# A joint activation-table set, doubled slot buffers, and half of one shared group moved behind the first experts

## The reference, cut to what matters

```python
x = x + tanh(g_xattn[0]) * attention(_layernorm(x), ctx)      # 16 heads, quantised, all 2048 tokens
x = x + tanh(g_ffn[0])   * moe0(_layernorm(x))                # 32 experts, 4 per token, shared part of width 704
x = x + tanh(g_xattn[1]) * wkv(time_decay, time_first, _layernorm(x), ctx)
x = x + tanh(g_ffn[1])   * moe1(_layernorm(x))                # 8 experts, 2 per token, shared part of width 352
```

## Time and profile before

| | us |
|---|---|
| median of 3 runs | 1297.46 (1297.25 to 1297.59) |
| the profiled execution | 1299.77 |
| its span, first to last instruction | 1298.0 |
| TensorE busy | 1081.6 (83% of the span) |
| VectorE busy | 969.6 (75%) |
| ScalarE busy | 899.4 (69%) |
| GpSimd busy | 696.8 (54%) |

### The profile page before, as it was taken

How to read it: one execution, slowest core, us unless ns; L and a number is a source line. 1 busy time by engine, 2 the same in 40 slices (tenths; PEclk the granted TensorE clock), 3 DMA queues, 4 the chain that set the end, 5 groups by cost and what they waited for, 6 DMA issues and landing times.

```text
span 1298.0 us, 24037 instructions
## 1 busy us (share of the span) xinstructions
PE 1081.6 (83%) x8245; PEld 631.3 (49%) x8360; DVE 969.6 (75%) x1781; ACT 899.4 (69%) x1537; POOL 696.8 (54%) x610
## 2 busy tenths in 40 slices
PE   6958888888888888888888875998998697798992
PEld 4623444444444444444444653565544254456771
DVE  6999899999999999999999567233235687643334
ACT  4649899999999999999999653144406465533441
POOL 3016988887887888788787615276301000462331
PEclk9969999999999999999999977999999898699996
DMA  5686787888897888886676454199431021123335
GB/s 173 125 143 127 155 179 161 158 176 169 165 173 164 171 165 181 167 170 124 114 115 108 73 167 135 31 278 265 159 121 65 0 79 55 41 85 98 97 97 205
DMA packets 388191, 176.36 MB, mean 136 GB/s; under 512 B 329805, under 2 KB 373042, under 8 KB 388072
## 3 DMA queue, kind: packets, MB, share of 16 engines
q1 hardware_dynamic: 381368, 157.84, 55.7%
q0 software_dynamic: 6480, 16.77, 3.9%
q10 hardware_dynamic: 224, 0.20, 0.0%
HBM read 52.70 MB, written 43.59 MB: 74 GB/s over the span
## 4 chain that ended last, share of the span: by engine, by line
PE 42%; DVE 31%; ACT 10%; issue 7%; DMA 5%; POOL 4%; SPq 1%; POOLq 0%; DVEq 0%; ACTq 0%
DVE top L368 20%; PE bank L217 7%; PE bank L231 7%; ACT weight L411 6%; PE bank L2340 4%; PE bank L1081 3%; DMA answered_rows<-yrow,target 3%; PE bank L249 3%; PE bank L1064 3%; PE bank L2356 2%; PE bank L1068 2%; PE bank L1721 1%; PE bank L267 1%; DVE x_sb L2028 1%; POOL weight L463 1%
## 5 line engine op out<-in xcount | busy, mean ns | idle before, releaser
L411 ACT ACTIVATE weight<-bank,bias,sq_all 128x1024 uint8<-128x1024 f32 x512 | 610.0, 1200 | 32.4 <-PE bank L231 27.2
L368 DVE TENSOR_REDUCE top<-bank 128x1 f32<-128x512 f32 (+1 forms) x683 | 610.8, 951 | 16.1 <-PE bank L217 5.0
L463 POOL CAST weight<-turned 128x2048 bf16<-128x2048 uint8 x256 | 478.9, 1892 | 45.2 <-PE bank L249 24.7
L231 PE MATMUL bank<-kT,query 128*128 128x512 bf16 x915 | 285.7, 384 | 26.2 <-ACT weight L411 12.2
L249 PEld LDWEIGHTS bank<-v_sb,weight 128*128 128x128 bf16 x4096 | 172.1, 97 | 109.7 <-POOL weight L463 7.4
L217 PE MATMUL bank<-kT,qspace 64*128 64x512 bf16 x687 | 138.1, 395 | 63.2 <-DVE top L368 63.2
L249 PE MATMUL bank<-v_sb,weight 128*128 128x16 bf16 x4096 | 172.6, 170 | 6.3 <-POOL weight L463 5.9
L217 PE MATMUL bank<-kT,query 128*128 128x512 bf16 x331 | 127.0, 384 | 2.1 <-DVE top L368 1.4
L1697 POOL DMA_INDIRECT dispatched_rows<-qspace,put x32 | 33.9, 1060 | 152.6 <-DVE qspace L2130 144.0
L231 PEld LDWEIGHTS bank<-kT,query 128*128 128x128 bf16 x1024 | 60.1, 97 | 104.2 <-ACT weight L411 60.6
L411 ACT ACTIVATION_READ_ACCUMULATOR weight<-bank,bias,sq_all 128x1 f32 x512 | 101.5, 198 | 0.0
(11 more groups left out here) (303 smaller groups left out, 1530.3 us busy)
## 6 DMA issues: line engine op xcount, KB each, us to landing
dispatched_rows<-zeros SPq DMA_DIRECT2D x32, 524.0 KB, 3.2
answered_rows<-zeros SPq DMA_DIRECT2D x16, 512.0 KB, 3.1
late<-answered_rows SPq DMA_DIRECT2D x16, 512.0 KB, 5.7
wgu<-in_L_ffn_w_gate SPq DMA_DIRECT2D x32, 176.0 KB
wgu<-in_L_ffn_w_up SPq DMA_DIRECT2D x32, 176.0 KB
wdn<-in_L_ffn_w_down SPq DMA_DIRECT2D x32, 176.0 KB
erow<-dispatched_rows SPq DMA_DIRECT2D x39, 131.0 KB
query<-qspace SPq DMA_DIRECT2D x32, 128.0 KB, 3.1
```

Source lines behind the costliest of these rows:

```text
L231: mm = pe.matmul(unit[u % 2][:, v * 512:(v + 1) * 512], query2[:, t % 2, h, :], kT[:, h // 2, first + v * 512:first + (v + 1) * 512], star ...
L368: ve.tensor_reduce(top[:, first:first + count], bank[:, first % 3:first % 3 + count, :], AX.X, ALU.max).then_inc(s_max, 1)
L411: ac.activation(weight8[:, n % BYTES, u * 1024:(u + 1) * 1024], unit[u], ACT.Exp, bias=bias[:, n:n + 1], scale=sq_all[:, n:n + 1], accum_o ...
L463: po.tensor_copy(weight[:, n % 3, :, :, :].rearrange("p c q two -> p (c q two)"), turned8[:, n % 3, :, :].rearrange("p c q -> p (c q)").bi ...
```

## The change

It has three parts.

1. `ac.preload_act_table_set("natural_log_exp_and_others")` is written into ScalarE's list at 14 places: once in the preparation behind the Tanh, twice in the front (behind chunks 0 and 1 of the shared part), eleven times in mixing, each behind the last Silu of a run. This set holds Ln and Exp both.
2. `marked` and `numbered` get a second buffer each, used in turn. `mark_slots(g)` waits for `table_products` g-1 instead of g, and from group 2 on only. `front_pool` does the same, and starts a group at `choices_marked` (the end of `choose`) instead of `destinations_ready` (the end of `place`).
3. Chunks 3 to 5 and the four answers of shared group 0 leave the front. They stand at the head of mixing now, before those of group 1, on TensorE, ScalarE and VectorE. The experts' TensorE list waits for `hidden_ready` 3 in place of `shared_answers_added` 4.

```diff
+            LOGS = "natural_log_exp_and_others"
@@ preparation, ScalarE
                     ac.activation(tgates[:], gates[:], ACT.Tanh).then_inc(s_prep_scalar, 1)
+                    ac.preload_act_table_set(LOGS)
                     triple(2)
@@ buffers
-            marked = late[:, 6, :].bitcast(BF16).rearrange("p (n s) -> p n s", s=P)
+            marked = [late[:, k, :].bitcast(BF16).rearrange("p (n s) -> p n s", s=P) for k in (6, 4)]
...
@@ front_pool
-                    po.wait_ge(sm_["destinations_ready"], g + 1)
-                    if g > 0:
-                        po.wait_ge(sm_["table_products"], g)
+                    po.wait_ge(sm_["choices_marked"], g + 1)
+                    if g >= 2:
+                        po.wait_ge(sm_["table_products"], g - 1)
@@ front_tensor
                 fill_table(3)
-                hidden0(0, 3, 6)
-                pe.wait_ge(sm_["rows_chosen"], 1)
-                answers0(0)
@@ front_scalar
                 shared_scalar(ac, 0, 0, 1)
+                ac.preload_act_table_set(LOGS)
                 copy_logits(2)
...
                 shared_scalar(ac, 0, 1, 2)
+                ac.preload_act_table_set(LOGS)
                 copy_logits(3)
...
                 residuals(3)
-                shared_scalar(ac, 0, 3, 6)
@@ mark_slots
-                    else:
-                        ve.wait_ge(sm_["table_products"], g)
+                    if g >= 2:
+                        ve.wait_ge(sm_["table_products"], g - 1)
@@ front_vector
                 mark_slots(3)
-                hidden0(0, 2, 5)
+                hidden0(0, 2, 3)
                 take_table()
-                hidden0(0, 5, 6)
-                answers0(0)
@@ experts_tensor
-                    pe.wait_ge(sm_["shared_answers_added"], G)
+                    pe.wait_ge(sm_["hidden_ready"], 3)
@@ mixing_tensor
                         pe.wait_ge(sx_["answers_weighted"], E0)
+                        for c in range(3, NW0):
+                            hidden0(0, c)
+                        for k in range(G):
+                            answers0(0, k)
                         for c in range(NW0):
                             hidden0(1, c)
@@ mixing_scalar (the first and two of the other ten preloads)
+                        shared_scalar(ac, 0, 3, NW0)
                         shared_scalar(ac, 1, 0, NW0)
                         for c in range(4):
                             shared_scalar(ac, 2, c, c + 1)
+                        ac.preload_act_table_set(LOGS)
...
                         shared_scalar(ac, 3, 1, 3)
+                        ac.preload_act_table_set(LOGS)
                         inverse(1)
...
                         silu1(1, 2)
+                        ac.preload_act_table_set(LOGS)
                         copy_rows(2)
```

More of the change, by code:

```diff
@@ L1128, in program @@
             table = buffers(first_experts)
-            marked = late[:, 6, :].bitcast(BF16).rearrange("p (n s) -> p n s", s=P)
-            numbered = late[:, 7, 0:G * K0 * E0].bitcast(BF16).rearrange("p (n a e) -> p n a e", a=2, e=E0)
+            marked = [late[:, k, :].bitcast(BF16).rearrange("p (n s) -> p n s", s=P) for k in (6, 4)]
+            numbered = [late[:, 7, k * G * K0 * E0:(k + 1) * G * K0 * E0].bitcast(BF16).rearrange("p (n a e) -> p n a e", a=2, e=E0) for k in range(2)]
             slot_b, slot_n, lane, lane_n = table("slot_b", [P, P], BF16), table("slot_n", [P, P], U32), table("lane", [P, 1]), table("lane_n", [P, 1], U32)
@@ L1160, in front_pool @@
                 for g in range(NG):
-                    po.wait_ge(sm_["destinations_ready"], g + 1)
-                    if g > 0:
-                        po.wait_ge(sm_["table_products"], g)
+                    po.wait_ge(sm_["choices_marked"], g + 1)
+                    if g >= 2:
+                        po.wait_ge(sm_["table_products"], g - 1)
                     for k in range(G):
                         n = slice(k * K0, (k + 1) * K0)
-                        po.tensor_scalar(numbered[:, n, 0, :], hot[:, g % 2, n, :], float(g * G + k + 1), None, ALU.mult).then_inc(sm_["slots_numbered"], 1)
-                    po.tensor_scalar(numbered[:, :, 1, :], hot[:, g % 2, :, :], lane[:, 0:1], None, ALU.mult).then_inc(sm_["slots_numbered"], 1)
+                        po.tensor_scalar(numbered[g % 2][:, n, 0, :], hot[:, g % 2, n, :], float(g * G + k + 1), None, ALU.mult).then_inc(sm_["slots_numbered"], 1)
+                    po.tensor_scalar(numbered[g % 2][:, :, 1, :], hot[:, g % 2, :, :], lane[:, 0:1], None, ALU.mult).then_inc(sm_["slots_numbered"], 1)
             def front_tensor(pe):
@@ L1208, in fill_table @@
                     for n in range(G * K0):
-                        mm = pe.matmul(bank[:, 7, 0:2 * E0], marked[:, n, :], numbered[:, n, :, :].rearrange("p a e -> p (a e)"),
+                        mm = pe.matmul(bank[:, 7, 0:2 * E0], marked[g % 2][:, n, :], numbered[g % 2][:, n, :, :].rearrange("p a e -> p (a e)"),
                                        start=g == 0 and n == 0, stop=g == NG - 1 and n == G * K0 - 1)
```

2 lines of the change are left out of this document (1 added, 1 removed).

## The result

The changed kernel took **1285.42 us** (median of 4 runs, 1284.8 to 1285.71) against 1297.53 for the kernel before beside it: ratio **0.9902**, 95% interval 0.9885 to 0.9919. The forecast was 1285.8.

What follows compares the result with a forecast made beforehand. The prediction took a chain of waits to bound the kernel, through TensorE for 42% and VectorE for 31%. Front, experts and moved work -4.2 and mixing -7.5 sum to -11.7, off the median 1297.46: 1285.8 us, range 1280.5 to 1292.5.

Steps and rivals of the forecast that it cites:

- The front's first loads: End of attention to choose(1): two table loads (2.57 us) and one before group 3's Exp (1.28) leave the chain, -3.85 us.
- the prediction's estimate was 1273: Rival: each of nine loads on the chain also costs a drain of 1.4 us, about 1273 us; chance 0.01.
- The table: Front: with second buffers and the earlier loads the table is full at 801.2 against 810.06, -8.9 us (bounds -7 and -10.3).
- Table to experts: Full table to first expert: TensorE idles 4.5 us and 1.2 for two gathers, cold clock +1.3; experts start 27.5 us earlier.
- Behind the experts: Moved chunks (10.4 us) and answers (0.89 and 11.97) stand in full on TensorE's chain after the experts: +23.3 us.
- The front net: Front, experts and moved work together: -27.5 + 23.3 = -4.2 us.
- Mixing: Loads leave ScalarE's chain around inverse(1), inverse(2), inverse(3), other loads stood in waits: -7.5 us, bounds -3.5 and -11.
- the clock, which the forecast kept as a rival at -3: Rival: shorter TensorE gaps in mixing keep its clock up, 3 us more gained, 1282.8 us; chance 0.13.
- GpSimd does not pace the experts: Rival claimed the opposite: GpSimd's lost lead of six gathers (7.8 us) shows in full, 1293.6 us; chance 0.14.
- Mixing does not swallow the loads: Rival claimed the opposite: VectorE is next in line in mixing, -3.5 instead of -7.5, 1289.8 us; chance 0.18.
- The experts don't stay cold: Rival claimed the opposite: first experts stay at 1.2 GHz, up to 2.6 us each, kernel slower; chance 0.03.
- The set is kept: Rival claimed the opposite: Ln and Exp still get their own sets, 14 loads added, none saved, 1299.7 us; chance 0.03.

Runs made afterwards that it cites:

- Experiment 5, e6_scalar_numbers: Changed kernel with the wide product of group 3's numbers on ScalarE instead of GpSimd: 0.9908 of the kernel before.
- e8, experiment 7: Joint set and buffers without the move, chunk 3 done ahead of fill_table(3), VectorE's chunk 2 ahead of place(3): 0.9842 of the kernel before.
- e10: Joint set and buffers without the move, run beside the changed kernel in one session: 1304.36 us, 0.9880 of the kernel before.

## Why the prediction was right, by its own steps

The total held (1285.8 against 1285.42), and so did the split in its main lines; the term for mixing was too small, and a fall of the clock behind the experts hid most of that by chance.

- **The front's first loads**, -3.85: measured -4.0 at `choose(1)`. No drain of 1.4 us per switch shows: Ln at 741.49 comes with VectorE's statistics, and the start is 2.62 us earlier, 1.28 of its own, as one load of 1.283 says. By the Trainium skill (ScalarE: Activation LUTs, "What ACT_TABLE_LOAD costs"), which counts a drain with every switch, the prediction's estimate was 1273. The total of 1285.42 doesn't bear that out.
- **The table**, -8.9: measured -9.0, but the step inside was told the wrong way round. The forecast let VectorE's `mark_slots(3)` wait for GpSimd's wide product. In fact `mark_slots` ran undelayed (2.29) and GpSimd's product stretched from 1.56 to 3.69. As one full wait is one full wait, the table was full at the same time. Experiment 5 shows that it is this wait: without the product GpSimd no longer sets the end.
- **Table to experts**, 4.5 and 1.2 us exposed, clock +1.3: measured 4.61 and 0.69 idle, and 1.1 on the first product (2.55 against 1.45). -28.3 against the forecast -27.5.
- **Behind the experts**, +23.3: measured +23.5 in four profiles (102.09 against 78.61). In the profiled run of the changed kernel it was 25.1, because the clock fell once at chunk 5 of group 2 (3.54 in place of 1.93 us); kernels without the move show such a fall too (`e8`, `e10`).
- **The front net**, -4.2: of its own -2.7 in this profile, -4.3 without that fall of the clock. It is made of -4.0 (loads), -4.2 to -5.0 (buffers, by the total of the run and by the table) and +4.3 (move).
- **Mixing**, -7.5: measured -9.8 over all profiles. The pieces taken from the chain held (-1.3, -1.4, -4.0). The step that was mis-sized is "the other loads stood in waits" and with it the clock, which the forecast kept as a rival at -3. Both are partly true: about 1.0 us of loads and 0.7 of clock between `copy_logits(0)` and `copy_logits(1)`, and 1.1 more than forecast behind `inverse(3)` (0.8 by the means over all profiles), which no run takes apart. Against it stands that `inverse(1)`'s second load brought 0.4 (0.2 by the means), not 1.3: for the same 105 matmuls TensorE was busy 26.54 us in place of 25.62 in that stretch, at a granted clock of 0.85 in place of 0.86.
- **The rivals.** GpSimd does not pace the experts (84.75 us with the earlier start; 82.2 to 84.6 in the profiles without the move at the same speed, and 93.31 against 92.14 in the third session: 2.6 us at most, not 7.8). Mixing does not swallow the loads. The experts don't stay cold: 0.79 over 806 to 812, then 1.00. (The prediction's sum for that rival is off: at 2.6 us each, five cold experts give 1298.8 and ten 1311.8, not 1300.) The set is kept: 19 loads fewer. That the sum came out within 0.4 us is partly luck: mixing's extra 2.3 stands against one fall of the clock behind the experts, 1.6.

What the prediction didn't weigh is that its own terms already said the move is a loss: 4.5 + 1.2 + 1.3 + 23.3 against the 25.65 between full table and first expert before is +4.6, and the run of the move alone measured +4.3. The net of -4.2 hid it, and no rival named it.

## What to carry to other kernels

Work that covers the latency of a gather should stay where it stands, unless something else can cover it: moving it behind the consumers cost the uncovered wait and a cold TensorE here, 4 us in all, and with one chunk left in the gap (two products of 1.72 us warm) the kernel with the move (0.9860) was as fast as the one without (0.9880, the intervals overlap). So sum each part of a joint change by itself, and drop the parts whose own sign is wrong. Table loads are to be counted on the chain, but loads that seem to stand in waits are not all free: between `copy_logits(0)` and `copy_logits(1)` such loads cost about 1.0 us, and TensorE's lower clock at the start of that stretch about 0.7. And where the chain goes through an instruction that doesn't need the table (a copy), place the preload behind it and not in front of it; here that gave 2.1 us.

## What the runs showed of the hardware that was not expected

- When `mark_slots` on VectorE (2.28 us) and a product on GpSimd overlap, it is GpSimd that is held: its wide product took 1.56 alone and 3.69 where it started 0.06 us ahead of `mark_slots` (794.91 and 794.97), and VectorE lost nothing. In experiment 7 the product started 0.96 us ahead and took 1.56, `mark_slots` 2.28:
```profile
797.05 1.56 POOL L1169 TENSOR_SCALAR late<-qspace,lane 128x512 bf16<-128x512 f32 x1
...
798.01 2.28 DVE L1391 TENSOR_TENSOR late<-slot_b,qspace 128x2048 bf16<-128x2048 bf16 x1
```
  ScalarE did the same product in 0.71 us during a `mark_slots`. The Trainium skill (SBUF — State Buffer, "Who interferes with whom") has such a pair shut each other out for the whole instruction, the one that issued first holding up the other. The length of the first case fits this (3.69 us, nearly 1.56 + 2.28), the order doesn't, unless 0.06 us is too little a lead to be read from these rows. In the second case the two overlap for 0.60 us and neither is longer than alone, which that rule doesn't lead one to expect.
- The same instructions behind the experts ran with and without a fall of the clock at chunk 5 of group 2: the stretch from the last answer row to `inverse(0)` took 78.61 (five profiles) or 80.26 and 81.49 without the move, and 102.09 (four) or 103.7 (two) with it. The wait ahead is the same. First the changed kernel, then `e6_scalar_numbers`:
```profile
979.39 3.54 PE L1070 MATMUL bank<-xT,sw 128*64 128x512 f32 x4 [2.33 <-DVE hT L1103]
```
```profile
989.10 1.93 PE L1070 MATMUL bank<-xT,sw 128*64 128x512 f32 x4 [2.33 <-DVE hT L1103]
```
  This makes 1.6 to 2.9 us of difference between like kernels, and is why a single profile can't weigh an edit of 1 us in the total.
- The sessions differ by 1.6%, most of it in the two stages of experts; ratios within a session carried over between them (0.9880 twice for the same kernel; 0.9902 and 0.9924 for the other).
